# Router logits of a decoder layer: from a stage of their own to 8 extra columns of the attention projections

## What is computed

```python
x = _layernorm(x + _L0_attn_ref(x, w_in, w_out))
x = _layernorm(x + _L0_xattn_ref(x, ctx, ctx, Wq, bq, Wk, bk, Wv, bv, Wo, bo))
probs = jax.nn.softmax(x @ Wr + br, axis=-1)      # Wr is 256 x 8
gates, ids = jax.lax.top_k(probs, 2)
...
x = _layernorm(x + _L0_ffn_ref(x, ...))
```

## Time and profile before

| | |
|---|---|
| median of 3 runs | 1739.3 us (1735.84 to 1740.15) |
| profiled execution | 1737.31 us, its span 1735.6 us |
| TensorE busy | 1463.6 us, 84% of the span |
| VectorE, ScalarE, GpSimd busy | 1054.5, 970.5, 632.2 us |
| mean granted TensorE clock | 0.924 of full speed |

### The profile page before, as it was taken

How to read it: one execution, slowest core, us unless ns; L and a number is a source line. 1 busy time by engine, 2 the same in 40 slices (tenths; PEclk the granted TensorE clock), 3 DMA queues, 4 the chain that set the end, 5 groups by cost and what they waited for, 6 DMA issues and landing times. The chain is left out here.

```text
span 1735.6 us, 43611 instructions
## 1 busy us (share of the span) xinstructions
PE 1463.6 (84%) x17896; PEld 1214.8 (70%) x17896; DVE 1054.5 (61%) x2277; ACT 970.5 (56%) x1419; POOL 632.2 (36%) x615
## 2 busy tenths in 40 slices
PE   5999999999999999999998591223999999999950
PEld 4777777777777777777776341223999999999950
DVE  3666666666667677767766347794544454455425
ACT  3677767777766666676765220012655555555507
POOL 1544444444432222322230000055254455454326
PEclk9999999999999999999999795555999999999985
DMA  5011112112112222222111341004334433442229
GB/s 178 20 57 57 57 57 63 58 56 68 45 52 67 75 75 75 74 74 75 63 60 38 126 116 12 0 0 134 83 58 96 97 81 61 96 98 45 28 53 357
DMA packets 129795, 129.54 MB, mean 75 GB/s; under 512 B 28288, under 2 KB 116464, under 8 KB 129600
## 3 DMA queue, kind: packets, MB, share of 16 engines
q1 hardware_dynamic: 114496, 106.29, 19.6%
q0 software_dynamic: 15104, 20.48, 7.1%
HBM read 82.54 MB, written 44.20 MB: 73 GB/s over the span
## 5 line engine op out<-in xcount | busy, mean ns | idle before, releaser
L495 ACT ACTIVATE at_pr<-at_A 128x2048 f32<-128x2048 f32 x128 | 240.7, 1880 | 196.4 <-PE at_A L325 196.4
L587 DVE TENSOR_REDUCE at_mx<-at_A 128x12 f32<-128x1536 f32 x128 | 224.6, 1755 | 32.7 <-PE at_A L292 27.1
L34 PE MATMUL ex_D<-ex_w,ex_hT 128*128 128x256 f32 (+1 forms) x1920 | 233.8, 281 | 0.4
L34 PEld LDWEIGHTS ex_D<-ex_w,ex_hT 128*128 128x128 f32 (+1 forms) x1920 | 230.5, 184 | 3.1 <-DVE ex_raw L1426 1.9
L34 PE MATMUL ex_U<-ex_xT,ex_w 128*128 128x384 f32 (+1 forms) x1152 | 222.1, 352 | 0.0
L1482 POOL DMA_INDIRECT total<-ex_o,ex_ids x80 | 131.6, 1645 | 228.0 <-DVE ex_o L1431 196.3
L34 PEld LDWEIGHTS ex_U<-ex_xT,ex_w 128*128 128x128 f32 x1152 | 207.2, 189 | 7.4
L716 POOL TENSOR_SCALAR_AFFINE_SELECT at_pr<-at_pr 128x2048 f32<-128x2048 f32 x64 | 128.5, 2008 | 225.2 <-ACT at_pr L495 225.2
L1416 DVE TENSOR_TENSOR ex_hT<-ex_h,ex_hT 128x384 fp32r<-128x384 f32 (+1 forms) x192 | 112.6, 587 | 97.0 <-ACT ex_hT L1376 97.0
L623 DVE TENSOR_TENSOR at_oT<-at_C,at_oT 128x512 fp32r<-128x512 f32 x64 | 44.3, 692 | 178.0 <-ACT at_oT L508 178.0
L325 PE MATMUL at_A<-at_qp,at_kt 32*128 32x256 f32 x2048 | 142.5, 392 | 0.0
(11 more groups left out here) (189 smaller groups left out, 2703.3 us busy)
## 6 DMA issues: line engine op xcount, KB each, us to landing
ex_w_in<-in_w SPq DMA_DIRECT2D x16, 1024.0 KB, 6.8
at_turned<-in_x_turned SPq DMA_DIRECT2D x16, 512.0 KB, 4.0
at_x<-in_x SPq DMA_DIRECT2D x16, 512.0 KB, 3.7
x<-at_y SPq DMA_DIRECT2D x32, 256.0 KB, 2.2
at_x<-x SPq DMA_DIRECT2D x16, 512.0 KB, 3.7
at_turned<-in_ctx_turned SPq DMA_DIRECT2D x16, 512.0 KB, 4.1
rows<-at_y SPq DMA_DIRECT2D x32, 256.0 KB, 2.2
total<-at_y SPq DMA_DIRECT2D x32, 256.0 KB, 2.8
```

Of the source, the lines that this page charges most:

```text
L34: last = nc.tensor.matmul(out, pick_l(left, a), pick_r(right, b), start=(start and n == 0), stop=(stop and n == 2))
L495: nc.scalar.activation(pr[:, k % 2].rearrange("p i n a q -> p (i n a q)"), A[:].rearrange("p i n a q -> p (i n a q)"), ACT.Exp).then_inc(e ...
L587: nc.vector.tensor_reduce(mx[:, k % 2, 0:12], A[:, 0:3].rearrange("p i n a k -> p (i n a) k"), AX, ALU.max).then_inc(max_done, 1)
```

## The change

The logits are linear in the row before the norm: (y - mean) times rstd, times Wr, is y times Wr with the mean of Wr's columns taken out, times rstd. So 8 columns go along. In the first layer the value matrix gets the 8 columns of the centred Wr (`wv` is 264 wide), whose products over the tokens are the residual's share; the output matrix gets Wo times Wr; for the second layer likewise, and the bias. The rows `x`, `y` and `x1` are 264 wide; `residual` adds the 8 columns too, and GpSimd scales them by rstd and writes `logits`. The stage `logits_block` is gone. `mean_of_wr` and `through_wr` make the columns once at the start; for that SyncE loads Wr, both Wo turned, and the bias, and writes the zero rows.

Two tiles of 264 columns don't fit one bank. So values and output are now written tile by tile, in turn into `B[0]` and `B[1]` (`project_v(g, n)`, `output(u, n)`), each with a wait of its own; q goes to `B[0]` and k to `B[1]`; values are copied in four pieces in place of two, the residual in two in place of one. At s = 3 VectorE takes the first two pieces ahead of `rest_o`, and the source of group g + 2 is split at s = 2 in place of s = 3.

```diff
-        x = sb("x", [P, XB, NB, D])
+        WX = D + E
+        x = sb("x", [P, XB, NB, WX])
...
+        y = sb("y", [P, 4, 2, WX])
...
+        wv = [sb(f"wv{i}", [P, 2, HALVES, WX], FP32R) for i in range(2)]
+        wo = [sb(f"wo{i}", [P, 2, HALVES, WX], FP32R) for i in range(2)]
...
@@ -204,7 +233,7 @@
 
                 if half == 0:
                     pe.wait_ge(x_loaded[g % XB], 16 * (g // XB + 1))
-                pe.wait_ge(v_done, 2 * g - 1 + half)
+                pe.wait_ge(v_done, 4 * (g - 1) + 3 + half)
...
                 last.then_inc(k_full, 1)
 
-            def project_v(g, i):
-                if i == 0:
-                    pe.wait_ge(k_done, 2 * g + 1)
+            def project_v(g, n):
+                if n == 0:
                     if g >= 2:
-                        pe.wait_ge(res_done, 2 * (g - 2) + 2)
+                        pe.wait_ge(res_done, 4 * (g - 2) + 4)
+                    else:
+                        pe.wait_ge(q_done, 2 * g + 2)
+                    if g == 0:
+                        pe.wait_ge(wr_ready, 1)
+                elif n == 1:
+                    pe.wait_ge(k_done, 2 * g + 2)
                 else:
-                    pe.wait_ge(k_done, 2 * g + 2)
-                b = B[i]
-                for j in range(2):
-                    n = 2 * i + j
-                    for t in range(HALVES):
-                        last = matmul3(nc, b[:, j * D:(j + 1) * D], source(g), wv[layer(g)], t == 0, t == HALVES - 1,
-                                       lambda x_, a, t=t: x_[:, a, t, n * P:(n + 1) * P],
-                                       lambda w_, a, t=t: w_[:, a, t, :])
+                    pe.wait_ge(v_done, 4 * g + n - 1)
+                b = B[n % 2]
+                width = D if cross(g) else WX
+                for t in range(HALVES):
+                    last = matmul3(nc, b[:, 0:width], source(g), wv[layer(g)], t == 0, t == HALVES - 1,
...
-            def output(u):
-                pe.wait_ge(ot_lo, u + 1)
+            def output(u, n):
                 g = u // 2
+                if n == 0:
+                    pe.wait_ge(ot_lo, u + 1)
+                if u == 0 and n == 0:
+                    pe.wait_ge(ext_ready, 1)
                 if u % 2 == 0:
                     if g + 2 < groups and cross(g + 2):
-                        pe.wait_ge(tx_lo, tx(g + 2, 0) + 1)
-                    pe.wait_ge(v_done, min(2 * (g + 1) + 1, 2 * groups))
-                    if g >= 1:
-                        pe.wait_ge(res_done, u)
+                        pe.wait_ge(tx_lo, tx(g + 2, n) + 1)
+                    elif g + 1 < groups:
+                        pe.wait_ge(v_done, 4 * (g + 1) + 3 + n)
+                    else:
+                        pe.wait_ge(res_done, 4 * (g - 1) + 4 - n)
+                elif g + 2 < groups:
+                    pe.wait_ge(k_done if n == 0 else q_done, 2 * (g + 2) + 1 + n)
                 else:
-                    pe.wait_ge(res_done, u)
-                    if g + 2 < groups:
-                        pe.wait_ge(k_done, 2 * (g + 2) + 1)
-                b = B[0]
-                for n in range(2):
+                    pe.wait_ge(res_done, 4 * g + 2 - n)
+                b = B[n if u % 2 == 0 else 1 - n]
+                for t in range(HALVES):
...
+            def mean_of_wr():
+                pe.wait_ge(wr_in, 16)
+                pe.wait_ge(zero_made, 1)
+                for t in range(HALVES):
+                    last = nc.tensor.matmul(C[1][:, 0:E], even[:], wr[:, t, :], start=(t == 0), stop=(t == HALVES - 1))
+                last.then_inc(mean_full, 1)
...
+            def through_wr():
+
+                pe.wait_ge(wr_ready, 1)
+                pe.wait_ge(ext_in, 48)
+                pe.wait_ge(bo_wide_done, 1)
+                b = C[1]
...
+                for place in range(5):
+                    lay, half = divmod(place, 2)
...
                     if g >= 1:
-                        output(2 * g - 2)
+                        output(2 * g - 2, 0)
+                        output(2 * g - 2, 1)
...
-            def take_v(g, i):
-                act.wait_ge(v_full, 2 * g + i + 1)
+            def take_v(g, n):
+                act.wait_ge(v_full, 4 * g + n + 1)
                 if g >= 2:
                     act.wait_ge(o_full, 4 * (g - 2) + 4)
-                nc.scalar.copy(v[:, g % 2, 2 * i:2 * i + 2, :, 0:DK],
-                               B[i][:, :].rearrange("p (n h d) -> p n h d", n=2, h=H)).then_inc(v_done, 1)
+                nc.scalar.copy(x[:, g % XB, n, D:WX], B[n % 2][:, D:WX])
+                nc.scalar.copy(v[:, g % 2, n, :, 0:DK], B[n % 2][:, 0:D].rearrange("p (h d) -> p h d", h=H)).then_inc(v_done, 1)
...
                     take_k(g + 1, 1)
+                    if g + 2 < groups:
+                        source_hi(g + 2)
                 elif s == 3 and more:
                     if not cross(g + 1):
-                        take_v(g + 1, 1)
-                    if g + 2 < groups:
-                        source_hi(g + 2)
-                        if cross(g + 2):
-                            turned_x_hi(g + 2, 0)
+                        take_v(g + 1, 2)
+                        take_v(g + 1, 3)
+                    if g + 2 < groups and cross(g + 2):
+                        turned_x_hi(g + 2, 0)
...
-                nc.vector.tensor_tensor(y[:, u % 4].rearrange("p n d -> p (n d)"), B[0][:, :],
-                                        x[:, g % XB, 2 * np_:2 * np_ + 2, :].rearrange("p n d -> p (n d)"),
-                                        ALU.add).then_inc(res_done, 1)
-                dve.wait_ge(res_done, u + 1)
+                for n in range(2):
+                    dve.wait_ge(out_full, 2 * u + n + 1)
+                    nc.vector.tensor_tensor(y[:, u % 4, n, :], B[n if np_ == 0 else 1 - n][:, 0:WX],
+                                            x[:, g % XB, 2 * np_ + n, :], ALU.add).then_inc(res_done, 1)
+                dve.wait_ge(res_done, 2 * u + 2)
...
+                if s == 3 and more and cross(g + 1):
+                    take_v(g + 1, 0)
+                    take_v(g + 1, 1)
                 if k % 2 == 1 and k >= 3:
                     rest_o((k - 3) // 2)
                 if s == 3 and more and cross(g + 1):
-                    take_v(g + 1, 0)
-                    take_v(g + 1, 1)
+                    take_v(g + 1, 2)
+                    take_v(g + 1, 3)
...
+                g, np_ = divmod(u, 2)
+                scale = rstd[:, u % 2, :].unsqueeze(2).to_broadcast([P, 2, E])
+                if cross(g):
+                    first = (g - layer_groups) * NB + 2 * np_
+                    nc.gpsimd.tensor_tensor(logits[:, first:first + 2, :], y[:, u % 4, :, D:WX], scale, ALU.mult).then_inc(logit_part, 1)
+                    pool.wait_ge(logit_part, u - 2 * layer_groups + 1)
+                    nc.gpsimd.tensor_tensor(logits[:, first:first + 2, :], logits[:, first:first + 2, :],
+                                            br[:].unsqueeze(1).to_broadcast([P, 2, E]), ALU.add)
+                else:
+                    nc.gpsimd.tensor_tensor(y[:, u % 4, :, D:WX], y[:, u % 4, :, D:WX], scale, ALU.mult)
                 nc.gpsimd.tensor_tensor(shift[:, u % 2, :], shift[:, u % 2, :], rstd[:, u % 2, :], ALU.mult).then_inc(shift_done, 1)
...
-                if s == 3 and g + 2 < groups:
+                if s == 2 and g + 2 < groups:
                     source_lo(g + 2)
...
-def logits_block(nc, tiles, rows_dram, sum_dram, wr_dram, br_dram, ident_dram, logits):
...
-        logits_block(nc, tiles, rows, total, ins["wr"], ins["br"], ins["ident"], logits)
+        attention_layers(nc, groups, ins["x"], ins["x_turned"], ins["ctx_turned"], x1, [rows[:, 0:D], total],
+                         {k: ins["attn_" + k] for k in ("wq", "wk", "wv", "wo", "wo_t")},
+                         {k: ins["xattn_" + k] for k in ("wq", "wk", "wv", "wo", "wo_t", "bq", "bk", "bv", "bo")},
+                         ins["wr"], ins["br"], logits, [rows[tokens:tokens + P, :], total[tokens:tokens + P, :]], ins)
```

More of the change, by code:

```diff
@@ L21 @@
 EPS = 1e-5
+E = 8
 def wait(eng, sem, value):
@@ L179, in _ @@
             sp.dma_start(bv[:], w_cross["bv"].rearrange("(a n) -> a n", a=1).to_broadcast([P, D])).then_inc(bias_in, 16)
-            sp.dma_start(bo[:], w_cross["bo"].rearrange("(a n) -> a n", a=1).to_broadcast([P, D])).then_inc(bias_in, 16)
+            sp.dma_start(bo[:, 0:D], w_cross["bo"].rearrange("(a n) -> a n", a=1).to_broadcast([P, D])).then_inc(bias_in, 16)
+            sp.wait_ge(zero_made, 1)
+            for rows in spare_rows:
+                sp.dma_start(rows, zero[:, 0:rows.shape[1]]).then_inc(zeroed, 16)
             for g in range(groups):
@@ L384, in output @@
                     for t in range(HALVES):
-                        last = matmul3(nc, b[:, n * D:(n + 1) * D], oT, wo[layer(g)], t == 0, t == HALVES - 1,
-                                       lambda o_, a, t=t, n=n: o_[:, u % 2, a, t, n * P:(n + 1) * P],
```

(21 more changed lines are left out.)

257 lines of the change are left out of this document (101 added, 156 removed).

## The result

| kernel | median us (lowest to highest) | ratio to before, 95% interval |
|---|---|---|
| before | 1738.49 (1735.84 to 1740.15, 4 runs) | |
| changed | 1760.24 (1759.59 to 1766.19, 4 runs) | 1.0134 [1.0108, 1.0160] |

The change costs 21.8 us (1760.24 - 1738.49; the ratio in the table is that of the mean times). The side was right and the size was not: I had said +9. The time lies in the range, in the part that I had given to another rival.

A forecast was written before the change was run, and what follows sets the result against it. TensorE's pace was taken to bound both attentions. -59.6 + 44.0 + 22.4 + 1.3 + 0.4 (last pair's norm) + 0.5 = +9.0 us on 1737.3 gave 1746.3, for the median 1748 us; range 1723 to 1768.

The forecast's parts named there:

- The stage that goes: Logits stage between the attentions and routing: nothing overlaps it, so all of it goes, -59.6 us.
- The new wait: Cross groups, second output tile at s = 0: TensorE waits for VectorE's low part of half 1, 16 times, +44.0 us.
- The clock behind it: TensorE after each new stall: the granted clock falls, costing 1.4 us each, 16 times, +22.4 us.
- The rival in which the clock holds: Cross part: the stall is there but TensorE stays at the upper clock level, 1726 us; chance 0.18.
- long low stretches: Behind each cross-part stall the low clock lasts 7 us, 3.1 in place of 1.4 us lost, 1775 us; chance 0.13.
- The source split: Self part, split moved from s = 3 to s = 2: wins TensorE's 3.7 us score bank wait; +1.3 with the wider columns.
- The cover on ScalarE and VectorE: Rival, self groups: value copies at s = 3 delay the score bank copy, up to 16 us more, 1764 us; chance 0.09.
- The self part: Sign for the self part: nothing changes by more than 0.3 us a group; if it grows, the prediction is wrong.
- The start: Program start: an extra load, column making and small products against earlier first maxima, between -2 and +5, taken as +0.5 us.

The follow-up runs named there:

- experiment 3: The changed kernel with GpSimd's low part of the source split, still at s = 2, issued as two instructions of half the size: 1761.0 us.
- experiment 2: The changed kernel with the source split back at s = 3: 1747.4 us with both parts back, 1744.5 us with only GpSimd's part back.

## Why the prediction was right and wrong

**The stage that goes**, -59.6: right. With both losses taken out the kernel stands at 1680.9, and 1738.5 - 59.6 is 1678.9; in the 2 us between lie the columns, the start and the 0.9 us waits that are left, less the gain from ScalarE's part. The profiles of before and after say it more directly: the last exponentials of the attentions start 83.3 us later (960.33 to 1043.67) and routing 22.2 later, so 61.2 us went between the two.

**The new wait**, +44.0: right. 16 waits, 45.6 + 2.9 = 48.5 us, less some 8.5 at `turn_x`, where the mean wait fell from 1.36 us (19.1 in 14) to 0.83 (12.5 in 15) and not to 1.1: about 40.

**The clock behind it**, +22.4: right, in its size partly by luck. 1.4 us in the timeline, 1.6 from the kernel with the stall alone. But I had halved the length of the low stretches with no row that said half. And I had argued that all three of them followed idle that was shorter in each piece than the new stall; for the one at 30 us that is false, since TensorE stood idle for 3.51 us in one piece before 28.59. For the other two it holds. Wait and clock together were 66.4 in my sum. They cost 76.0 put into the kernel before, and their removal from the changed kernel gave 1744.5 - 1680.9 = 63.6. The rival in which the clock holds fell with this, and so did the one with long low stretches.

**The source split**: this step failed. I wrote that the split "takes a ScalarE operation away from in front of a score bank copy" and "I take that as won", +1.3 for it and the columns together. The split is two instructions on two engines, and I priced one. ScalarE's part won about what I said: 2.9 us in the changed kernel and 7.9 in the kernel before, where I had 3.7. GpSimd's part I gave no price at all, because GpSimd was half idle and nobody waited for it; but it moved from the end of s = 3, where it reached only 0.25 us into the cast, onto the cast of another set. It cost 15.7 us. With that added, my +9.0 becomes +24.7 against 21.8 measured; the 2.9 us that are left are near the uncertainty between two sets of runs, and I can't ascribe them.

The profile of before held the warning. The cast's row there:

```profile
L595 DVE CAST at_m<-at_mx x127: 174/176/1155, 32.1 to 954.7; 128x16 bf16<-128x16 f32 x127
```

An operation with a minimum of 174, a median of 176 and a maximum of 1155 ns, on data of one size, is sometimes held by something. I read means only. The longest one, with the operation behind it, stands in the timeline of before, beside GpSimd's split of the cross weights (`split_cross`):

```profile
75.07 1.27 POOL L737 TENSOR_TENSOR at_wq<-at_w_cross_in,at_wq 128x512 fp32r<-128x512 f32 x1
75.22 1.16 DVE L595 CAST at_m<-at_mx 128x16 bf16<-128x16 f32 x1
76.30 1.28 POOL L737 TENSOR_TENSOR at_wk<-at_w_cross_in,at_wk 128x512 fp32r<-128x512 f32 x1
76.40 1.21 DVE L597 TENSOR_TENSOR at_m<-at_mx,at_m 128x16 bf16<-128x16 f32 x1
```

The cast ends with the first GpSimd instruction (76.38 and 76.34), the subtraction with the second (77.61 and 77.58). The outcome of experiment 3 could have been read here before anything was run. And in 12 self groups of before the cast took 0.27 us, its start covered by the last 0.25 us of the very instruction that I moved.

**The cover on ScalarE and VectorE**: the rival gave 1764, near the result, with 0.09. Its mechanism is refuted by experiment 2: ScalarE's copies cost nothing, and the free third of both engines did cover them. What it should have said is that free time on an engine doesn't protect it against a neighbour.

**The self part**, where "nothing changes by more than 0.3 us a group": it was +1.0, and a growth of the self part was one of the signs that I had named for being wrong. From the first exponentials to those of the fifteenth group it lost 13.7 us, where my terms for it, columns and split, come to -0.4. The wide columns alone stay inside the 0.3: with ScalarE's part early and GpSimd's late, a self group takes 28.26 us in the changed kernel and 28.13 in the kernel before. 48 matmuls of 4.3 ns, 0.2 us, were expected.

**The start**, +0.5: the first exponentials are 1.3 us later (34.06 to 35.37), inside the -2 to +5 that I had given.

Left open: how short a stall must be for the clock to stay up. Waits of 1.35 us before, and two or three of 0.9, kept it at 0.99 to 1.00; 2.2 us gave 0.97, 2.4 gave 0.94 to 0.97, 3.0 gave 0.94 to 0.96. But the length of one stall is not all: in the kernel before, the clock fell near 944.5, behind a wait of 1.55 us and within the next one, of 1.33; and at 968.5 it fell behind one of 2.02.

## What to carry to other kernels

When an edit moves a step, list its instruction on every engine and look at what runs beside each one at the new place, on the neighbour that shares memory with it as well; a busy share says nothing of that, while the maximum of a short operation far above its median does. A stall of TensorE cost its length here, 3 us, and about half as much again where the clock fell; work that needs nothing late, such as the weighting of the set before, can go into it: the wait of 0.88 us went whole. And where a bank is cut from two tiles to one, the order of its readers decides, more than their length.

## What the runs showed that I had not expected

VectorE's cast of 16 columns took 2.16 us under a GpSimd instruction of 2.36, and the same engine's reductions of 1536 and 512 elements beside the same instruction took their usual 1.76 and 0.69. Cutting the GpSimd instruction in two only handed the second half to the next small operation.

The lower clock came up to two groups of matmuls after the stall (746.97 against 745.81). The Trainium skill, TensorE: Matmul & The Clock Gate, section What's actually happening, says that the clock is lower after the engine has been idle for a while. The stalls of 3.04 and 2.42 us fit that. The first fall of the earlier trace rows shows that it needn't be one long wait: TensorE waited 1.55 us, worked for 1.2 and waited 1.33, and the granted clock went from 1.00 to 0.50.
